# One block for three parts: routing of the last part placed inside attention's tail, weights loaded early, filler products at a seam

## The chip, the cores and the metric

The kernel runs on one core of one Trainium2 chip. The metric is the device time of one execution in microseconds (us), lower is better; the time before is the median of three runs. TensorE (PE) does matrix products and transposes, VectorE (DVE), ScalarE (ACT) and GpSimd (POOL) do elementwise work and reductions, and SyncE (SP) issues DMAs; POOL also issues DMAs. Each engine works off its own instructions in the order in which they are written, and waits on semaphores for the others.

## The reference, cut to what matters

4,096 tokens of 256 numbers pass through an expert half-step, an attention-like block, and a second expert half-step with the same weights. Cut from the reference (`ln` is a layer norm; the second line's block works on the normed rows of four sequences of 1,024):

```
x = x + 0.5 * ffn(ln(x));  x = x + attn(ln(x));  x = x + 0.5 * ffn(ln(x))

ffn(t): logits = t @ gate_w + gate_b; probs = softmax(logits)      # [4096, 8]
        e = argmax(probs)                                           # one of 8 experts
        pos = how many tokens before this one chose e               # cumsum of the one-hot mask
        keep = pos < 160                                            # capacity of an expert
        out = keep * prob_e * (gelu(t @ w1[e] + b1[e]) @ w2[e] + b2[e])

attn(x): q, k, v, g = x @ Wq, Wk, Wv, Wg; a = complex(x @ Wa) -> sigmoid(|a|) * exp(i*angle(a))
         h = scan over time: h_t = a_t * h_(t-1) + k_t * v_t;  y = (q * h * silu(g)) @ Wo
         y = ln(y + x);  out = ln(gelu(y @ W1 + b1) @ W2 + b2 + y)
```

A token's place in its expert needs the choices of all tokens ahead of it, so routing runs from the first token to the last.

## The kernel before, in words

Three functions run one after the other: `expert_half_step` (turn 0, part 1), `attention` (part 2), `expert_half_step` (turn 1, part 3). Each opens a `nc.Block` of its own and an object `Semaphores`; at its end stand a barrier over all engines, the clearing of the part's semaphores, and another barrier. The end of each engine's program in a part is a branch.

**An expert part.** Tokens lie in 32 tiles of 128 (`NT`), the slots of eight experts in ten tiles (`ST`; 8 x 160 = 1,280). Routing: DVE takes each token's best expert (`choose`: `mask`, and `seen`, a running count per partition by a scan). PE turns these into counts of earlier tokens (`count`, into `bank[3]`). DVE makes slot numbers (`place`: row within a slot tile, `row_f`; slot tile, `hot_a`; `val_tok`, the token's number at its slot tile) and then `hot`, a one-hot matrix of rows per token tile in bf16. PE sums token numbers into slots, one product per token tile (`list_tokens`), DVE makes of that the index `idx_g`, and POOL gathers ten tiles of 128 rows from DRAM by indirect DMA. In the same way mean and rstd of each row, split into three bf16 parts (`row_split`, `val_row`), go through PE into slots (`list_rows`). The gathered rows are normed (DVE), transposed (PE), and each expert takes an up-product (`up`, 32 matmuls) and a down-product (`down`, 32 matmuls). `xo` is row plus half of the gated result, and POOL scatters it into the destination by indirect DMA (the fifth and last line of the loop at L533; then POOL waits for the scatters to land).

Part 1 routes in two groups of 16 tiles, the first while later rows still load; part 3 routes all 32 tiles at once. `keep_busy(n)` issues n products of 128x512 whose result nobody reads. Part 1's second route has 10, 14, 7 and 5 of them around count and lists, part 3's route has 8, 30, 8 and 5 (L824).

**Weights.** Each expert's 2 MB lie in one of four ring slots; SP loads expert e once the down-product of e-4 is done. At part 3, expert 0 has been loaded by attention's SP program, experts 1 to 3 are loaded at part 3's own start.

**Attention.** Eight blocks (`NB`) of 512 tokens, each in two quarters of 256 for the last stages. A hand-written table of (block offset, step, number) sets the order of the work; every engine walks it and issues those of its instructions that belong to a step. `LAST_STEPS` is its end. There the last block's second stages run alone: output product `wo`, `mix_stats` and `mix_norm` (layer norm: DVE statistics, POOL's `power` chain of small operations at L1107 to L1114, DVE again), `up`, `gelu`, `split`, `down`, `out_stats`, `out_norm`, and `next_turn` and `logits`, which already make part 3's gate logits for a quarter of rows. DVE's last instruction in attention is the logits of tiles 30 and 31. L1135 is a POOL operation of `mix_norm` that adds the bias to the residual rows. The first load of attention, `zb` of `x_mid` at L1064, follows the barrier, as do seven memsets on POOL, of which the last (`rsz`) lets all other engines begin (`par_ready`). The first PE work is `z_turn` (L1530, eight transposes), then projections (L1520 to L1522).

**On-chip memory** of part 3 lay where attention's tiles had been.

## Time and profile before

| | |
|---|---|
| median of 3 runs (735.6, 735.71, 1278.68) | 735.71 us |
| profiled execution | 737.4 us, span 735.6 us |
| mean granted clock of TensorE | 0.949 |
| busy: PE, DVE, ACT, POOL | 638.0 (87%), 472.7 (64%), 453.5 (62%), 194.8 us (26%) |
| part 1 ends on DMA, POOL's last scatter | 139.59 us + landing |
| attention ends, last logits on DVE | 620.7 us |
| part 3: first filler, first expert product, last work | 624.0, 646.4, 730.9 us |

The times in the rows count from the span's start. In a timeline row stand start, busy time, engine, line, operation, output<-input, shape and count; the bracket is the idle time ahead of it and what ended that. In the windows, `PEclk` is the TensorE clock that was granted, as a share of 2.4 GHz; 0.50 is 1.2 GHz. The rows are in a section of their own below.

### The profile page before, as it was taken

What the parts mean: (1) busy time and instruction counts of PE and PEld (TensorE: products, weight loads), DVE (VectorE), ACT (ScalarE), POOL (GpSimd) and SP (SyncE); (2) the same over time, 40 slices, a digit from 0 to 9 for tenths busy, and PEclk for the clock granted to TensorE, in tenths of its full rate; (3) what the DMA queues carried; (4) which work ended last, traced back from release to release, by engine and by line L of the source; (5) the groups of instructions that cost most, each with busy time, mean ns of one, the idle gap of its engine ahead of it and who ended that gap; (6) DMA issues with size and microseconds to landing.
All of it is one profiled execution on the core that took longest, in us unless ns stands there. A gap on an engine that the chain in (4) does not pass through costs nothing. (4 is left out here: it accounts for less than half of the span.)

```text
span 735.6 us, 11483 instructions
## 1 busy us (share of the span) xinstructions
PE 638.0 (87%) x4252; PEld 566.3 (77%) x4252; DVE 472.7 (64%) x1037; ACT 453.5 (62%) x814; POOL 194.8 (26%) x289
## 2 busy tenths in 40 slices
PE   6989899456879899999999899999985995989995
PEld 3458899335668889889899798898885895479994
DVE  5664500135697989989989989988899453630001
ACT  3325334037779889898898898897896251144440
POOL 6141001221013123334234226214242221230112
PEclk9999999859879999999999999999997898899999
DMA  6939891050101201202220221011011130915720
GB/s 203 341 125 389 273 333 43 32 180 29 57 30 58 73 1 45 72 6 68 72 66 11 69 72 44 29 44 44 1 44 43 41 133 18 359 53 170 253 79 25
DMA packets 48816, 74.07 MB, mean 101 GB/s; under 512 B 4614, under 2 KB 40539, under 8 KB 48696
## 3 DMA queue, kind: packets, MB, share of 16 engines
q1 hardware_dynamic: 44408, 59.84, 24.6%
q0 software_dynamic: 4352, 13.49, 5.2%
q8 instruction: 34, 0.56, 0.3%
q14 instruction: 22, 0.18, 0.1%
HBM read 62.45 MB, written 15.20 MB: 106 GB/s over the span
## 5 line engine op out<-in xcount | busy, mean ns | idle before, releaser
L1520 PE MATMUL bank<-zt_h,w_in_h 128*128 128x512 f32 x192 | 81.1, 423 | 14.4 <-DVE qg L1207 6.1
L903 PE MATMUL bank<-xdt,ring 128*128 128x160 f32 x512 | 75.8, 308 | 5.3 <-DMA ring<-in_L_ffn_w 4.3
L1520 PE MATMUL bank<-yt_h,w_h 128*128 128x256 f32 x256 | 74.3, 290 | 6.9 <-DVE yt_l L1317 5.9
L903 PEld LDWEIGHTS bank<-xdt,ring 128*128 128x128 f32 x512 | 73.4, 197 | 6.0 <-DMA ring<-in_L_ffn_w 4.5
L1521 PE MATMUL bank<-zt_l,w_in_h 128*128 128x512 f32 x192 | 77.0, 401 | 0.0
L711 DVE SCALAR_TENSOR_TENSOR xo<-bank,gate,xg 128x256 f32<-128x256 f32 x20 | 9.2, 481 | 105.5 <-PE bank L930 105.5
L1522 PE MATMUL bank<-zt_h,w_in_l 128*128 128x512 f32 x192 | 76.8, 400 | 0.0
L1520 PE MATMUL bank<-w_h,ht_h 128*128 128x256 f32 x256 | 74.2, 290 | 0.0
L916 PE MATMUL bank<-hid,ring 128*128 128x160 f32 x512 | 72.8, 300 | 1.5 <-DVE idx_s L695 0.7
L1521 PE MATMUL bank<-w_l,ht_h 128*128 128x256 f32 x256 | 72.2, 282 | 0.0
L1522 PE MATMUL bank<-w_h,ht_l 128*128 128x256 f32 x256 | 72.2, 282 | 0.0
L916 PEld LDWEIGHTS bank<-hid,ring 128*128 128x128 f32 x512 | 70.4, 190 | 2.3 <-issue 2.3
L1521 PE MATMUL bank<-yt_l,w_h 128*128 128x256 f32 x256 | 72.1, 282 | 0.0
L1522 PE MATMUL bank<-yt_h,w_l 128*128 128x256 f32 x256 | 72.1, 282 | 0.0
L747 ACT ACTIVATE hid<-bank,b1t 128x160 f32<-128x160 f32 x128 | 50.4, 393 | 31.3 <-PE bank L903 18.3
L1107 POOL TENSOR_TENSOR rsq<-mvq,eps_ln 128x2 f32<-128x2 f32 x32 | 13.8, 430 | 208.8 <-DVE mvq L1168 208.8
L1494 ACT ACTIVATE hf<-bank,b_t 128x256 f32<-128x256 f32 x128 | 53.3, 468 | 18.2 <-PE bank L1522 13.4
L1520 PEld LDWEIGHTS bank<-zt_h,w_in_h 128*128 128x128 f32 x192 | 37.4, 195 | 25.3 <-DVE qg L1207 7.9
L1520 PEld LDWEIGHTS bank<-yt_h,w_h 128*128 128x128 f32 x256 | 48.9, 191 | 10.1 <-DVE yt_l L1317 8.0
L756 ACT ACTIVATE eot<-bank,b2t 128x160 f32<-128x160 f32 x32 | 12.6, 393 | 60.3 <-PE bank L916 60.3
L1521 PEld LDWEIGHTS bank<-yt_l,w_h 128*128 128x128 f32 x256 | 48.9, 191 | 0.7
L1521 PEld LDWEIGHTS bank<-w_l,ht_h 128*128 128x128 f32 x256 | 48.7, 190 | 0.4
(238 smaller groups left out, 1599.8 us busy)
## 6 DMA issues: line engine op xcount, KB each, us to landing
ring<-in_L_ffn_w SPq DMA_DIRECT2D x32, 1024.0 KB, 8.9
xc<-in_L_attn_x SPq DMA_DIRECT2D x8, 512.0 KB, 4.4
zb<-x_mid SPq DMA_DIRECT2D x8, 512.0 KB, 4.5
z_mid<-zb POOLq DMA_DIRECT2D x8, 512.0 KB, 3.4
zr<-z_mid SPq DMA_DIRECT2D x16, 256.0 KB, 2.8
xr<-x_mid SPq DMA_DIRECT2D x16, 256.0 KB, 3.6
out<-xq POOLq DMA_DIRECT2D x16, 256.0 KB, 4.2
xc<-in_L_attn_W SPq DMA_DIRECT2D x4, 512.0 KB, 8.4
```

The source lines that it names most:

```text
L711: V.scalar_tensor_tensor(xo[:, a % GT, :], bank[6 + a % 2][:, 0:D], gate[:, a:a + 1], xg[:, a, :], ALU.mult, ALU.add).then_inc(xo_ready, 1)
L747: S.activation(hid[:, e % 2, m, :], bank[b][:, 0:CAP], ACT.Gelu_apprx_tanh, bias=cst["b1t"][:, e * KF + m:e * KF + m + 1]).then_inc(gelu_d ...
L756: S.activation(eot[:, d, slots(e)], bank[4 + d][:, 0:CAP], ACT.Identity, bias=cst["b2t"][:, e * KD + d:e * KD + d + 1]).then_inc(eo_done, 1)
L903: ins = T.matmul(bank[b][:, 0:CAP], w1_of(s)[:, k, m * P:(m + 1) * P], xdt[:, k, e * CAP:(e + 1) * CAP], start=k == 0, stop=k == KD - 1)
L916: ins = T.matmul(bank[4 + d][:, 0:CAP], w2_of(e % GE)[:, m, d * P:(d + 1) * P], hid[:, e % 2, m, :], start=m == 0, stop=m == KF - 1)
L1107: own.step(G.tensor_tensor(rs[:], mv[:, :, 1], cst[eps][:, 0:n], ALU.add))
L1494: ins = S.activation(hf[m % 2][:, t, :], upb[m % 2][:, t * QW:(t + 1) * QW], ACT.Gelu_apprx_tanh, bias=b1_t[:, 2 * m + t:2 * m + t + 1])
L1520: T.matmul(out, left[0], right[0], start=start, stop=False)
L1521: T.matmul(out, left[0], right[1], start=False, stop=False)
L1522: return T.matmul(out, left[1], right[0], start=False, stop=stop)
```

## The change

All three parts stand in one `nc.Block`, without barriers between them. Each engine goes from its last instruction of a part to its first of the next.

- **First seam.** Attention's first load on SP waits for the five scatter semaphores of part 1 in place of the barrier. PE issues 30 fillers, waits for that load (`z_in[0]`), and issues 12 more ahead of the first transposes. POOL clears part 1's semaphores once, behind its first `z_norm` DMA.
- **Routing of part 3** is cut into tiles 0 to 25 (`EARLY`) and 26 to 31. For the first 26 the steps `choose`, `place`, `hot` and `rows` on DVE and `count`, `list_tokens` and `list_rows` on PE are new entries in `LAST_STEPS`: each takes the next piece of part 3's program, which is a generator (`yield`). The last six tiles, 26 to 31, are the second group, routed behind the last logits, with 8, 10, 4 and 5 fillers in place of 8, 30, 8 and 5.
- **Weights.** Part 3's four ring slots are now in memory that attention's first stages have left, so SP issues the loads of experts 0 to 3 behind a wait for the last block's `yg_done`, 2 MB each. What attention still uses lies below a spacer (`live`).
- Banks for counts, lists and fillers in part 3 are others than in part 1.

PE at the first seam (L916/L992 down, L930/L1006 turn_out, L1530/L1634 transposes). Before:

```order
L916 MATMUL bank<-hid,ring_0 128x160 x8
L930 MATMUL bank<-ident,eot 128x128 x4
L279 UNCONDITIONAL_BRANCH
L1513 UNCONDITIONAL_BRANCH
L1530 MATMUL bank<-ident,zb 128x128 x8
L1520 MATMUL bank<-zt_h,w_in_h 128x512
L1521 MATMUL bank<-zt_l,w_in_h 128x512
```

and now:

```order
L992 MATMUL bank<-hid,ring_0 128x160 x8
L1006 MATMUL bank<-ident,eot 128x128 x4
L1607 UNCONDITIONAL_BRANCH
L1621 MATMUL bank<-iota_p,ones_h 128x512 x42
L1634 MATMUL bank<-ident,zb 128x128 x8
L1614 MATMUL bank<-zt_h,w_in_h 128x512
L1615 MATMUL bank<-zt_l,w_in_h 128x512
```

The two branches (end of a part, start of the next) are one, and 42 fillers (L1621; 30, the wait for the load, 12) stand ahead of the transposes.

PE at the end of attention (L1607/L1608: the last product's residual; `xq`: transposes of `next_turn`; `gate_c`: logits; L814/L818: count; L834: lists). Before:

```order
L1608 MATMUL bank<-ident_r,yt_l 128x128
L1617 MATMUL bank<-ident,xq 128x128 x4
L1625 MATMUL bank<-gate_c,x3t 128x8 x4
L951 UNCONDITIONAL_BRANCH
L764 UNCONDITIONAL_BRANCH
L824 MATMUL bank<-iota_p,ones_h 128x512 x8
L814 MATMUL bank<-mask,before_m 128x256
L818 MATMUL bank<-seen,ones_h 128x256
L824 MATMUL bank<-iota_p,ones_h 128x512 x30
L834 MATMUL bank<-val_tok,hot 128x20 x32
L824 MATMUL bank<-iota_p,ones_h 128x512 x8
L834 MATMUL bank<-xo,hot 128x60 x32
```

and now:

```order
L1712 MATMUL bank<-ident_r,yt_l 128x128
L906 MATMUL bank<-val_tok,hot 128x20 x26
L906 MATMUL bank<-xo,hot 128x60 x26
L1721 MATMUL bank<-ident,xq 128x128 x4
L1729 MATMUL bank<-gate_c,x3t 128x8 x4
L895 MATMUL bank<-iota_p,ones_h 128x512 x8
L885 MATMUL bank<-mask,before_m 128x48
L887 MATMUL bank<-seen,ones_h 128x48
L889 MATMUL bank<-seen,ones_h 128x48
L895 MATMUL bank<-iota_p,ones_h 128x512 x10
L906 MATMUL bank<-val_tok,hot 128x20 x6
L895 MATMUL bank<-iota_p,ones_h 128x512 x4
```

Both lists of 26 tiles (L906) stand ahead of the last four transposes; behind the logits the branches are gone, and count (L885 to L889), fillers (L895) and lists are short.

DVE between the statistics of the last quarter's mix and those of the first quarter's output. Before:

```order
L1305 TENSOR_TENSOR vn<-bank,zr 128x512
L1164 BN_STATS stq<-vn 128x6 x2
L1166 MEMSET spare_w 128x1
L1168 BN_AGGR mvq<-stq 128x2 x2
L1164 BN_STATS stq<-bank 128x6 x2
L1166 MEMSET spare_w 128x1
L1168 BN_AGGR mvq<-stq 128x2 x2
L1336 SCALAR_TENSOR_TENSOR xq<-bank,mvq,ln2s_b 128x256 x2
```

and now:

```order
L1250 BN_AGGR mvq<-stq 128x2 x2
L656 TENSOR_TENSOR eot<-mask,bank 128x208
L657 TENSOR_REDUCE r_1<-eot 128x26
L658 TENSOR_SCALAR r_1<-r_1 128x26
L659 TENSOR_TENSOR r1i_1<-r_1 128x26
L660 TENSOR_SCALAR r1i_1<-r1i_1 128x26
L661 TENSOR_TENSOR r_1<-r1i_1,r_1 128x26
L662 SCALAR_TENSOR_TENSOR row_f<-r1i_1 128x26
L663 TENSOR_TENSOR eot<-tile_no,r_1 128x260
L665 TENSOR_TENSOR val_tok<-eot,tok 128x520
L1246 BN_STATS stq<-bank 128x6 x2
L1248 MEMSET spare_w 128x1
```

`place` for 26 tiles, nine operations (L656 to L665), stands between the two; `choose`, `hot` and `rows` stand in the same manner at three other places.

The diff, cut to its core:

```diff
-ROUTES = (((0, NT // 2), (NT // 2, NT)), ((0, NT),))
+EARLY = NT - 6
+LIVE = 4576
+ROUTES = (((0, NT // 2), (NT // 2, NT)), ((0, EARLY), (EARLY, NT)))
+ROWS = (((0, NT // 2), (NT // 2, NT)), ((0, EARLY), (EARLY, NT)))
...
+    (-1, "choose", 0), (-1, "mix_norm", 0), (-1, "mix_turn", 0), (-2, "out_stats", 1), (-1, "wo", 1),
...
+    (-1, "gelu", 3), (-1, "split", 3), (-1, "count", 0), (-1, "mix_stats", 1), (-1, "place", 0),
+    (-2, "next_turn", 1), (-1, "down", 0), (-1, "mix_norm", 1), (-1, "mix_turn", 1), (-1, "out_stats", 0),
...
+    (-1, "gelu", 5), (-1, "split", 4), (-1, "next_turn", 0), (-1, "split", 5), (-1, "hot", 0), (-1, "up", 6),
+    (-1, "up", 7), (-1, "gelu", 6), (-1, "logits", 0), (-1, "split", 6), (-1, "down", 1), (-1, "list_tokens", 0),
+    (-1, "list_rows", 0), (-1, "gelu", 7), (-1, "split", 7), (-1, "rows", 0), (-1, "out_stats", 1),
+    (-1, "out_norm", 1), (-1, "next_turn", 1), (-1, "logits", 1),
...
+        sems, sems_first = ctx.enter_context(Semaphores(nc)), Semaphores(nc)
+        block = ctx.enter_context(nc.Block())
+        first = expert_half(nc, 0, sems_first, xf, x_mid, xf, (ln1_s, ln1_b, b1), bank, cst, ring0, gate_w, gate_b, ew1,
...
+        @block.vector
+        def _(v):
+            for _ in first.vector(v):
+                pass
+        @block.tensor
+        def _(pe):
+            for _ in first.tensor(pe):
+                pass
+        def second():
+            return expert_half(nc, 1, sems, outf, outf, None, None, bank, cst, ring0, gate_w, gate_b, ew1, eb1, ew2,
+                               eb2, None, None)
...
+        if not first:
+            sb("live", [P, LIVE], F32)
+        hot = sb("hot", [P, NT * P], BF16)
...
+        tok_bank, row_bank, spare_bank = (bank[2], bank[0], bank[1]) if first else (bank[0], bank[1], bank[2])
+        count_bank = [bank[3] if first else bank[0], bank[3]]
...
-            for e in range(0 if first else 1, NE):
+            for e in range(NE):
...
-                for t in range(*ts, CT):
+            def make_hot(b, ts):
+                for g in groups(ts):
+                    n = g[1] - g[0]
+                    V.tensor_tensor(hot_group(g), cst["iota_p"][:, :, 0:n],
+                                    row_f[:, g[0]:g[1]].unsqueeze(1).to_broadcast([P, P, n]),
                                     ALU.is_equal).then_inc(hot_ready, 1)
+            def make_rows(ts):
+                for g in groups(ts):
+                    val_parts(val_row, g, slice(0, 6)).then_inc(row_val, 1)
+            def list_ids():
+                v.wait_ge(list_ready, 1)
+                own.link(V.reduce_sum(ids[:], tok_bank[:, 0:2 * ST].rearrange("p (v a) -> p a v", a=ST), AX))
+                V.tensor_copy(idx_g[:], ids[:]).then_inc(idx_ready, 1)
...
-            for b, ts in enumerate(routes):
-                if first and b:
-                    row_logits(b, ts)
-                if not first or b:
-                    choose(b, ts)
-                place(b, ts)
-                row_split(ts)
-                if b == last:
-                    v.wait_ge(list_ready, 1)
-                    own.link(V.reduce_sum(ids[:], bank[2][:, 0:2 * ST].rearrange("p (v a) -> p a v", a=ST), AX))
-                    V.tensor_copy(idx_g[:], ids[:]).then_inc(idx_ready, 1)
-                for t in range(*ts, CT):
-                    val_parts(val_row, (t, t + CT), slice(0, 6)).then_inc(row_val, 1)
+            else:
+                choose(0, routes[0])
+                yield
+            place(0, routes[0])
+            yield
+            make_hot(0, routes[0])
+            yield
+            if routes[0] in rows:
+                row_split(routes[0])
+                make_rows(routes[0])
+            yield
+            if first:
+                row_logits(1, routes[1])
+            choose(1, routes[1])
+            place(1, routes[1])
+            make_hot(1, routes[1])
+            if routes[1] in rows:
+                row_split(routes[1])
+            for ts in rows:
+                if ts not in routes:
+                    row_split(ts)
+            list_ids()
+            for ts in rows:
+                if ts not in routes[:-1]:
+                    make_rows(ts)
...
             def keep_busy(n):
-                    T.matmul(bank[1][:], cst["ones_h"][:], cst["iota_p"][:, 0:BT // CT, :].rearrange("p a b -> p (a b)"),
-                             start=True, stop=True)
+                    T.matmul(spare_bank[:], cst["ones_h"][:],
+                             cst["iota_p"][:, 0:BT // CT, :].rearrange("p a b -> p (a b)"), start=True, stop=True)
...
+                    for k, g in enumerate(parts):
+                        if t == g[0]:
+                            pe.wait_ge(ready, k + 1)
                     ins = T.matmul(out, hot_of(t), val(t), start=t == 0, stop=t == NT - 1)
                 if ts[1] == NT:
...
             else:
+                count(0, routes[0])
+                yield
+                list_tokens(routes[0])
+                yield
+                list_rows(rows[0])
+                yield
                 keep_busy(8)
-                count(0, routes[0])
-                keep_busy(30)
-                list_tokens(0, routes[0])
-                keep_busy(8)
-                list_rows(0, routes[0])
+                count(1, routes[1])
+                keep_busy(10)
+                list_tokens(routes[1])
+                keep_busy(4)
+                list_rows(rows[1])
             keep_busy(5)
...
+                if is_first(b):
+                    sems_first.clear()
...
+        ctx.close()
+        last = second()
+        block.gpsimd(last.gpsimd)
...
+                if is_first(b):
+                    for k in range(GT):
+                        sp.wait_ge(scattered[k], 16 * NG)
+                sp.dma_start(zb[b.par][:], rows).then_inc(z_in[b.par], 16)
...
+            run(sp, dict(load_z=load_z, load_quarter=load_quarter), Chain(sp, gps), 0)
+            sp.wait_ge(yg_done, 2 * NB)
+            last.sync(sp)
...
+            half = last.vector(v)
+            def choose(b, j):
+                v.wait_ge(lgq_done, 2 * (NB - 1) - (1 if EARLY < (NB - 1) * JT else 0))
+                next(half)
+            def half_step(b, j):
+                next(half)
             per_block = (2 * JT - 1) + 10 * KD
             per_quarter = (2 * QT - 1) + (3 * QT - 2) + (3 * QT - 2)
-            run(v, dict(z_stats=z_stats, z_low=z_low, fold=fold, size=size,
+            run(v, dict(choose=choose, place=half_step, hot=half_step, rows=half_step, z_stats=z_stats, z_low=z_low, fold=fold, size=size,
...
+            v.wait_ge(lgq_done, 2 * NB)
+            for _ in half:
+                pass
...
+            def keep_busy(n):
+                for _ in range(n):
+                    T.matmul(o_ffn[:], cst["ones_h"][:], cst["iota_p"][:, 0:BT // CT, :].rearrange("p a b -> p (a b)"),
+                             start=True, stop=True)
             def z_turn(b, j):
+                if is_first(b):
+                    keep_busy(30)
+                    pe.wait_ge(z_in[0], 16)
+                    keep_busy(12)
...
+            half = last.tensor(pe)
+            def half_step(b, j):
+                next(half)
             run(pe, dict(z_turn=z_turn, project=project, wo=wo, mix_turn=mix_turn, up=up, down=down,
-                         next_turn=next_turn, logits=logits), Chain(pe, actc), 0)
+                         next_turn=next_turn, logits=logits, count=half_step, list_tokens=half_step,
+                         list_rows=half_step), Chain(pe, actc), 0)
+            for _ in half:
+                pass
```

## Rows read from the trace of the kernel before

**Rows 1.** Chain that ended last, part 3's head: start us, us, what.

```profile
637.60 0.18 DVE idx_g L671
...
640.11 4.87 DMA xg<-out,idx_g
...
646.43 6.29 PE bank L903 x32
```

**Rows 2.** Timeline, PE, fillers of part 3: start us, us, what, count.

```profile
623.97 3.57 PE L824 MATMUL bank<-iota_p,ones_h 128*128 128x512 bf16 x8 [3.75 <-PEq L218]
...
637.13 1.89 PE L824 MATMUL bank<-iota_p,ones_h 128*128 128x512 bf16 x8
```

**Rows 3.** Timeline, DVE, attention's tail: last bracket is idle before, and releaser.

```profile
581.17 0.76 DVE L1164 BATCH_NORM_STATS2 stq<-bank 128x6 f32<-128x256 f32 x2 [5.64 <-PE bank L1608]
...
597.56 0.76 DVE L1164 BATCH_NORM_STATS2 stq<-bank 128x6 f32<-128x256 f32 x2 [3.32 <-PE bank L1608]
...
607.59 0.36 DVE L1364 SCALAR_TENSOR_TENSOR logits<-bank,mean_rstd,gate_b_sb 128x8 f32<-128x8 f32 x2 [1.89 <-PE bank L1625]
...
614.38 0.76 DVE L1164 BATCH_NORM_STATS2 stq<-bank 128x6 f32<-128x256 f32 x2 [5.23 <-PE bank L1608]
...
620.32 0.36 DVE L1364 SCALAR_TENSOR_TENSOR logits<-bank,mean_rstd,gate_b_sb 128x8 f32<-128x8 f32 x2 [1.81 <-PE bank L1625]
```

**Rows 4.** DMA issues of 80 to 190 us: what, count, median us to landing.

```profile
x_mid<-xo,idx_s POOLq DMA_INDIRECT x10, 2.4
```

**Rows 5.** Timeline, POOL, first seam.

```profile
139.59 0.98 POOL L533 DMA_INDIRECT x_mid<-xo,idx_s  x1 [0.30 <-issue]
...
145.99 0.10 POOL L1103 MEMSET rsz<- 128x4 f32 x1
```

**Rows 6.** Timeline, SP, first seam.

```profile
145.34 0.37 SPq L1064 DMA_DIRECT2D zb<-x_mid  x1
```

**Rows 7.** Timeline, PE, first seam, attention's transposes and first projections.

```profile
154.13 2.07 PE L1530 MATMUL bank<-ident,zb 128*128 128x128 f32 x8 [16.90 <-ACT zb L1388]
158.07 0.79 PE L1520 MATMUL bank<-zt_h,w_in_h 128*128 128x512 f32 x1 [1.87 <-DVE zt_l L1192]
...
162.06 0.40 PE L1520 MATMUL bank<-zt_h,w_in_h 128*128 128x512 f32 x1
```

**Rows 8.** Half-microsecond windows: us, PE, PEld, DVE, ACT, POOL busy, PEclk, DMA share, GB/s.

```profile
629.50:630.00 0.50, 0.50 (x4) 0.22 (x2) 0.43 (x4) 0.00 (x0) 0.00 (x0) 0.84 1.10 389
```

**Rows 9.** Timeline, DVE, part 1's second route of 16 tiles.

```profile
36.37 0.29 DVE L591 TENSOR_REDUCE r<-logits 128x16 f32<-128x128 f32 x1
...
38.16 0.42 DVE L601 TENSOR_TENSOR_SCAN seen<-not_first,mask 128x128 bf16<-128x128 f32 x1
...
39.77 0.29 DVE L609 TENSOR_TENSOR eot<-mask,bank 128x128 f32<-128x128 bf16 x1 [1.12 <-PE bank L818]
...
42.05 1.22 DVE L621 TENSOR_TENSOR hot<-iota_p,row_f 128x2048 bf16<-128x2048 bf16 x1
...
44.81 0.17 DVE L671 CAST idx_g<-ids 128x10 int32<-128x10 f32 x1
```

**Rows 10.** Timeline, PE, part 1's second lists and first expert product.

```profile
43.33 1.16 PE L834 MATMUL bank<-val_tok,hot 128*128 128x20 bf16 x16 [0.57 <-DVE hot L621]
...
51.62 4.58 PE L903 MATMUL bank<-xdt,ring 128*128 128x160 f32 x32 [0.56 <-ACT xdt L739]
```

**Rows 11.** Timeline, PE, attention's tail.

```profile
617.50 0.66 PE L1617 MATMUL bank<-ident,xq 128*128 128x128 f32 x4 [3.16 <-DVE xq L1348]
```

**Rows 12.** Timeline, POOL, late attention.

```profile
547.16 1.08 POOL L1107 TENSOR_TENSOR rsq<-mvq,eps_ln 128x2 f32<-128x2 f32 x1 [7.45 <-DVE mvq L1168]
...
594.32 0.20 POOL L1107 TENSOR_TENSOR rsq<-mvq,eps_ln 128x2 f32<-128x2 f32 x1 [7.48 <-DVE mvq L1168]
...
595.66 1.29 POOL L1135 TENSOR_TENSOR xr<-xr,ln2b_b 128x512 f32<-128x512 f32 x1
```

**Rows 13.** Two-microsecond windows, same columns, part 1's first product.

```profile
50.00:52.00 2.00, 0.82 (x5) 0.61 (x6) 1.75 (x6) 0.71 (x2) 1.70 (x2) 1.00 0.61 127
```

More of the change, by code:

```diff
@@ L210, in new, with clear @@
         return self.all[-1]
+    def clear(self):
+        self.nc.clear_and_free_semaphores(self.all)
+        self.all = []
     def __enter__(self):
@@ L288, in expert_half_step @@
         ring = [ring0] + [sb(f"ring{s}", [P, WE], F32) for s in range(1, GE)]
+        eot = sb("eot", [P, KD, GS], F32)
+        xo = sb("xo", [P, GT, D], F32)
+        mask, seen = sb("mask", [P, NT * NE], BF16), sb("seen", [P, NT * NE], BF16)
+        top, best, base, pos, late, tile_f, total, prob = [sb(f"r1{k}", [P, NT], F32) for k in range(8)]
         xg = sb("xg", [P, ST, D], F32)
@@ L893, in up @@
                 s = e % GE
-                loads = e // GE + (0 if s == 0 and not first else 1)
-                if loads:
-                    pe.wait_ge(w_in[s], loads * 32)
+                pe.wait_ge(w_in[s], (e // GE + 1) * 32)
                 pe.wait_ge(xdt_ready, -(-(e + 1) * CAP // P))
```

161 lines of the change are left out of this document (72 added, 89 removed).

## The prediction

> **What bounds the kernel now.** The table of busy time comes first: TensorE (PE) is busy 87% of the span and VectorE (DVE) 64%, so what PE does in the steady part is not touched by this change, and only places where PE waits or runs fillers can give time back. Then the chain of waits at part 3's head [rows 1]: the index `idx_g` is ready at 637.60 + 0.18 = 637.78 us, the gather beside it takes 4.87 us, and the first expert product starts at 646.43. Then the PE timeline there [rows 2]: from 623.97 on PE issues products nobody reads. Attention's last DVE instruction ends at 620.32 + 0.36 = 620.68 [rows 3]. So from 620.68 to 646.43, 25.75 us, nothing of the result is computed by PE; the length is that of barrier, route (17.1 us to the index) and gather (8.65 us from there to the first product). The first seam is the second such place: the last scatter is issued at 139.59 and lands some 2.4 us later, at 142.0 [rows 4, 5], SP's load follows at 145.34 [rows 6], and PE begins again at 154.13 [rows 7].
>
> **First seam.** The load leaves at about 142.1 in place of 145.34 (3.2 us earlier), and the last of POOL's memsets, which lets the others go, 0.75 us behind it as before (145.99 + 0.10 against 145.34 [rows 5, 6]), at 142.85. Load, norm and all up to the transposes took 154.13 - 145.34 = 8.8 us; without fillers the transposes would start at 150.9. But 42 fillers stand ahead of them. A filler takes 0.44 us at half clock, where eight took 3.57, and 0.23 at full, where eight took 1.89 [rows 2]. How long PE is at half clock after an idle stretch is between 3.9 us (158.07 to 162.06, the product's time falls from 0.79 to 0.40 [rows 7]) and 5.7 us (623.97 to about 629.66, worked out from the mean clock of 0.84 in the window that starts at 629.50 [rows 8]). I take 5.5, since here too PE starts from a long idle stretch into fillers: 12.5 fillers at 0.44 and 29.5 at 0.23 are 12.3 us, to 155.15. The fillers, not the load, then set the transposes: these take 1.04 in place of 2.07 at full clock, to 156.2, where they ended before as well. What is won is the clock of what follows: nine products that took 3.99 us [rows 7] take 9 x 0.23 = 2.1. **-1.9 us**; with 3.9 us of half clock it is -2.7.
>
> **Attention's tail.** DVE gets four pieces, each ahead of a wait that it had anyway [rows 3, 9]. `choose` with its scan took 38.16 + 0.42 - 36.37 = 2.2 us for 16 tiles, some 2.8 for 26, into an idle stretch of 5.64. `place` took 42.05 - 39.77 = 2.28 for 16, some 2.8, into 3.32. `hot` took 1.22 for 16, so 2.0, into 1.89. `rows` is an estimate: 1,560 elements at the rate of `hot` (1.22 for 2,048) are 0.95, and a dozen small operations near 0.17 each 2.0, together 3.0 to 3.1, into 5.23. In all 10.7 us into 16.1 us of idle time. Releasers stay the same, PE results in all four. PE gets a count and 52 list products; 16 took 1.16 us [rows 10], so 52 take 3.5, into an idle stretch of 3.16 ahead of 617.50 [rows 11]: 0.3 too long.
>
> POOL gets nothing, but runs beside `place`. Its small operation took 0.20 us with DVE idle and 1.08 beside DVE work [rows 12]; the chain of four that `mix_norm` waits for can so grow by up to 2.3 us of 3.32 that DVE had free, and DVE's own work can be held by the 1.29 us of L1135, which comes just behind [rows 12]. Nothing to 2.0 us for the whole tail; I take **+0.6**, 0.3 for PE and 0.3 for this, because most of the slower chain lies in the same stretch that `place` fills.
> The Trainium skill, "SBUF — State Buffer", section "Who interferes with whom", says that a VectorE instruction with two SBUF inputs contends with a GpSimd instruction that reads SBUF, and that the later of the two is fully blocked. By that rule the two-input operations of `place` and L1135 would add up instead of overlapping, and the sum below would be about 1 us higher; by the rows alone with no clash it would be 0.3 lower. The trace agrees with the rule as far as the 0.20 and the 1.08 go.
>
> The loads of experts 0 to 3, 8.4 MB, run at 389 GB/s in the window of 629.50 [rows 8], 21.5 us, and start behind the last block's `yg_done`, which lies between the mix statistics of its two quarters, 581.17 and 597.56 [rows 3]: they end between 603 and 619, before anything of part 3 reads them. Their DMA time lies beside attention's tail, which has only the output stores then. I take zero; the rival below prices it.
>
> **Second seam.** From DVE's last logits at 620.68 there is now a route of six tiles. The nearest rows are part 1's second route, of 16: 36.37 to 44.98, 8.6 us, with count and list in the same order [rows 9]. I take off 0.6 for `choose` and scan and 0.6 for `place` (a quarter each: ten of sixteen tiles are gone, but small operations hardly shrink), 0.7 for `hot`, 0.7 for ten list products at 0.07 [rows 10], and 0.4 of the 1.12 that DVE waited for the count behind ten half-clock fillers [rows 9]: 5.6 us, index at 626.3. From the index to the first product part 1 took 51.62 - 44.98 = 6.64 us [rows 9, 10], part 3 before 8.65 with ring loads beside the gather; those are gone. First product at 632.9 in place of 646.43: **-13.5**. It took 6.29 us there [rows 1] and 4.58 in part 1 [rows 10], where the clock was full [rows 13]. PE now has lists in place of the idle stretch ahead of 617.50, no barrier, and fillers as in part 1, so I take part 1's: **-1.7**.
>
> Behind it all work is the same. **Sum**: -1.9 + 0.6 - 13.5 - 1.7 = -16.5; 737.4 - 16.5 = 720.9 for the profiled execution. The median of the runs, 735.71, lies 1.7 below that execution: **719.2 us**. A measurement of this kernel tells about 2% from no change, that is anything below 721.0 or above 750.4.
>
> **Rivals.**
> - *The clock drops ahead of the first product all the same.* Between gather and product PE has nothing but four transposes, as before. Costs the 1.7: 720.9. Part 1 speaks against it, part 3 before for it.
> - *Half clock already in the short route.* If PE enters the eight fillers at 0.44 each they last 3.5 in place of 1.9 us, and the ten behind the count 4.4 in place of 2.3; both then end behind DVE: up to +3.3, 722.5. Before, PE was at half clock here, behind its idle stretch and the barrier; with lists in the stretch I doubt it.
> - *The loads disturb the tail.* 21.5 us at full DMA rate lie beside the last quarters' loads and stores; one quarter's load doubled would hold `mix` by some 3.5 to 4 us: 723.
> - *DVE's idle time is not idle when the pieces come.* The idle stretches are waits on PE, and if PE in turn waits for DVE's pieces, all 10.7 us come on top of what was taken as 0.6: 729.3. Against it: each piece stands ahead of a wait for a PE result that doesn't need the piece.
> - *PE stays at half clock through the 42 fillers.* They then last 18.5 us, transposes and nine products stay slow: +7.2 + 1.9, 728.3.
> - *Slower than before.* PE is busier at both seams, and if the chip answers with more half clock in attention, each stretch of 5.5 us at 1.2 GHz loses half, 2.75 us. Seven more of them (one per steady block) are 19.3: 738.5. It decides from six on (16.5 us). Nothing in the steady rows calls for it.
> - That the change does not do what it says would need `choose` to be held by logits of tile 25 that come late; they belong to the block before, so I give it nothing of its own.
>
> **How the numbers follow.** Forecast 0.44 (own range 716.8 to 721.5), drop ahead of the product 0.22, half clock in the route 0.12, loads 0.08, DVE not hidden 0.07, fillers at half 0.04, slower 0.03. With every small term at its good end (-0.8 at the first seam, no slip, 1 us less route) it is 716.8; with the index-to-product time of before (+2.0), the tail's full 2.0 and the drop of 1.7 it is 724.3, and a little more where the half-clock route joins one of them. Range 716.5 to 725.5; the last three cases lie outside. Below 721.0: nearly all of the forecast, half of the drop case, little else: 0.55. Above 750.4 only a heavier form of the slower case, 0.01.
>
> **What would show it.** First seam: fillers whose eighth part is 0.44 then 0.23, transposes from about 155 with no idle ahead of them, and nine products of 0.23. Tail: DVE pieces of 2.8, 2.8, 2.0, 3.1 with idle left behind the first and last; the last logits within a microsecond of before, counted from the transposes. Second seam: index 5.6 us behind the logits, gather under 4.87, product 6.6 behind the index and 4.6 long at granted clock 1.00. The prediction is wrong if the last logits come over 2 us late, if DVE waits for the count behind fillers, or if the product waits for weights.

## The result

The changed kernel takes 725.44 us (median of four, 724.42 to 725.73) against 736.07 (median of four): ratio 0.9844, 95% interval 0.9827 to 0.9862. One of the four executions of the kernel before, 1278.68 us, was in a slow state and is left out of the ratio and its interval. A second measurement (f1 below) gave 0.9882 (0.9850 to 0.9914). So it is faster, by 1.6% here and 1.2% there, but not by the 2% forecast as a little more likely than not: 719.2 us was predicted, a gain of 16.5, and 10.6 were won. The profiled execution has a span of 723.9 us, 11.7 less than before.

**First seam after the change.** PE's timeline (start, busy time, instruction, count, idle time ahead and its end), then POOL's last scatter of part 1 and SP's load:

```profile
135.75 0.66 PE L1006 MATMUL bank<-ident,eot 128*128 128x128 f32 x4 [0.48 <-ACT eot L828]
142.19 10.78 PE L1621 MATMUL bank<-iota_p,ones_h 128*128 128x512 bf16 x42 [5.79 <-POOL rsz L1143]
152.81 1.04 PE L1634 MATMUL bank<-ident,zb 128*128 128x128 f32 x8
155.81 0.50 PE L1614 MATMUL bank<-zt_h,w_in_h 128*128 128x512 f32 x1 [1.97 <-DVE zt_l L1274]
...
157.98 0.39 PE L1614 MATMUL bank<-zt_h,w_in_h 128*128 128x512 f32 x1
```

```profile
138.77 0.99 POOL L581 DMA_INDIRECT x_mid<-xo,idx_s  x1 [0.30 <-issue]
```

```profile
141.15 0.37 SPq L1212 DMA_DIRECT2D zb<-x_mid  x1
```

They answer to [rows 5, 6, 7]. The load leaves 2.38 us behind the issue of the last scatter; before, with barrier, clearing and barrier between them, it was 5.75 (139.59 to 145.34). The 42 fillers last 10.6 us up to the transposes, not 12.3; these last 1.04 us, as worked out. The nine products from the first projection to the tenth take 2.17 us (155.81 to 157.98) in place of 3.99. From the end of part 1's last transposes (136.41) to the start of the tenth product (157.98) it is 21.57 us; before it was 24.83 (137.23, the end of the transposes there, to 162.06).

**Attention's tail.** DVE's timeline, for [rows 3]:

```profile
577.80 0.76 DVE L1246 BATCH_NORM_STATS2 stq<-bank 128x6 f32<-128x256 f32 x2 [2.12 <-PE bank L1712]
...
592.40 1.28 DVE L662 SCALAR_TENSOR_TENSOR row_f<-r1i 128x26 bf16<-128x26 int32 x1
...
594.80 0.75 DVE L1246 BATCH_NORM_STATS2 stq<-bank 128x6 f32<-128x256 f32 x2
...
611.62 0.76 DVE L1246 BATCH_NORM_STATS2 stq<-bank 128x6 f32<-128x256 f32 x2 [2.17 <-PE bank L1712]
...
617.82 0.36 DVE L1446 SCALAR_TENSOR_TENSOR logits<-bank,mean_rstd,gate_b_sb 128x8 f32<-128x8 f32 x2 [2.06 <-PE bank L1729]
...
621.29 0.20 DVE L656 TENSOR_TENSOR eot<-mask,bank 128x48 f32<-128x48 bf16 x1 [1.50 <-PE bank L889]
...
625.01 0.17 DVE L685 CAST idx_g<-ids 128x10 int32<-128x10 f32 x1
```

`place` (its seventh operation, L662, stands in the second row) now fills the whole idle stretch, and the statistics behind it (594.80) start with no idle time ahead; `choose` leaves 2.12 and `rows` 2.17 us. In the route DVE waits 1.50 us for the count. PE's timeline there, for [rows 1, 2, 11]:

```profile
611.42 1.76 PE L906 MATMUL bank<-val_tok,hot 128*128 128x20 bf16 x26
613.04 1.77 PE L906 MATMUL bank<-xo,hot 128*128 128x60 bf16 x26
...
616.09 1.62 PE L1729 MATMUL bank<-gate_c,x3t 128*128 128x8 f32 x8 [0.69 <-ACT x3t L1600]
617.56 3.57 PE L895 MATMUL bank<-iota_p,ones_h 128*128 128x512 bf16 x8
...
621.08 3.37 PE L895 MATMUL bank<-iota_p,ones_h 128*128 128x512 bf16 x10
...
631.38 7.28 PE L979 MATMUL bank<-xdt,ring 128*128 128x160 f32 x32 [0.56 <-ACT xdt L811]
```

The eight fillers take 3.57 us, as at half clock before, and the first expert product 7.28. The windows of two microseconds (busy time of PE, PEld, DVE, ACT, POOL, then the granted clock, DMA share, GB/s) show why:

```profile
614.00:616.00 2.00, 1.40 (x18) 1.11 (x16) 1.68 (x7) 0.56 (x1) 0.89 (x2) 1.00 0.00 0
616.00:618.00 2.00, 1.91 (x10) 1.64 (x11) 0.18 (x2) 1.69 (x3) 0.84 (x3) 0.60 0.37 131
618.00:620.00 2.00, 2.00 (x6) 0.70 (x5) 1.59 (x9) 1.26 (x2) 0.00 (x0) 0.50 0.02 4
...
624.00:626.00 2.00, 1.89 (x20) 1.00 (x18) 1.22 (x6) 0.00 (x0) 0.53 (x1) 1.00 0.00 0
...
630.00:632.00 2.00, 1.31 (x4) 0.94 (x5) 1.83 (x8) 0.38 (x1) 1.39 (x3) 0.51 0.36 107
...
634.00:636.00 2.00, 2.00 (x9) 2.00 (x8) 0.29 (x1) 0.68 (x2) 1.42 (x2) 0.50 0.28 86
```

TensorE falls to 1.2 GHz within 616 to 618, is back at 2.4 by 624, and is low again in 630 to 636, through most of the first product.

**POOL beside `place`.** POOL's timeline, for [rows 12]:

```profile
591.38 0.69 POOL L1151 TENSOR_TENSOR rsq<-rsq,minus_half 128x2 f32<-128x2 f32 x1
...
592.30 1.33 POOL L1177 TENSOR_TENSOR xr<-xr,ln2b_b 128x512 f32<-128x512 f32 x1
```

Its chain is as quick as alone (0.69 us for the power operation), but L662 on DVE, which takes 0.18 for the same 26 tiles in f1 below, starts at 592.40 and ends at 593.68, just when L1177 (L1135 before) ends, at 593.63. In f1, the changed kernel again, L1177 starts a little earlier against DVE's sequence, and it is the operation ahead, L661, that is long:

```profile
591.71 1.29 POOL L1177 TENSOR_TENSOR xr<-xr,ln2b_b 128x512 f32<-128x512 f32 x1
```

```profile
591.71 1.33 DVE L661 TENSOR_TENSOR r<-r1i,r 128x26 f32<-128x26 int32 x1
592.96 0.18 DVE L662 SCALAR_TENSOR_TENSOR row_f<-r1i 128x26 bf16<-128x26 int32 x1
```

The same pair is there in all twelve executions with `place` in the tail: in six L661 is the long one, in six L662 (L663 and L664 in c1 to c3, e4, f2, f3). `choose` met it as well: its L646 ran beside the L1177 of the quarter before and took 1.19 us, but there 2.12 us of idle time were left behind it.

**The end.** POOL's last scatter:

```profile
715.77 0.99 POOL L581 DMA_INDIRECT out<-xo,idx_s  x1 [0.30 <-issue]
```

It is 7.14 us from its end to the end of the span at 723.9; before, it was 4.7 (735.6 less 730.9).

### The profile page after: what moved, and what is told of

It is laid out like the page before. It is cut to its first block and busy times, and to the rows that moved or that the text cites. A ratio compares the mean times of both kernels' runs of the same rounds, so it can differ in the third digit from the quotient of the medians.

```text
span 723.9 us, 11485 instructions
## 1 busy us (share of the span) xinstructions
PE 645.6 (89%) x4273; PEld 571.0 (79%) x4273; DVE 478.0 (66%) x1061; ACT 454.1 (63%) x815; POOL 196.8 (27%) x291
## 5 line engine op out<-in xcount | busy, mean ns | idle before, releaser
L979 PE MATMUL bank<-xdt,ring 128*128 128x160 f32 x512 | 77.4, 312 | 1.7 <-ACT xdt L811 1.1
L979 PEld LDWEIGHTS bank<-xdt,ring 128*128 128x128 f32 x512 | 75.0, 201 | 2.5 <-issue 1.7
L992 PE MATMUL bank<-hid,ring 128*128 128x160 f32 x512 | 72.8, 300 | 1.5 <-DVE idx_s L768 0.7
L992 PEld LDWEIGHTS bank<-hid,ring 128*128 128x128 f32 x512 | 70.4, 190 | 2.3 <-issue 2.3
```

Source lines behind the costliest of these rows:

```text
L979: ins = T.matmul(bank[b][:, 0:CAP], w1_of(s)[:, k, m * P:(m + 1) * P], xdt[:, k, e * CAP:(e + 1) * CAP], start=k == 0, stop=k == KD - 1)
L992: ins = T.matmul(bank[4 + d][:, 0:CAP], w2_of(e % GE)[:, m, d * P:(d + 1) * P], hid[:, e % 2, m, :], start=m == 0, stop=m == KF - 1)
```

## Where the time went: six stretches in all runs

Each number is a difference of rows like those above: **seam**, end of part 1's last transposes on PE to the start of attention's tenth product; **attention**, on to the end of DVE's last logits; **route**, on to the end of the cast to `idx_g`; **gather**, on to the start of the first expert product; **product**, its own time; **end**, from the end of PE's last transposes to the end of the span. All in us, one profiled execution each. What is not in a column, from the first product to PE's last transposes, is 74.7 to 74.8 us in every row but e3, where it is 78.3.

| run | part 1 | seam | attention | route | gather | product | end | span |
|---|---|---|---|---|---|---|---|---|
| before | 137.23 | 24.83 | 458.62 | 17.09 | 8.66 | 6.29 | 8.07 | 735.6 |
| changed | 136.41 | 21.57 | 460.20 | 7.00 | 6.20 | 7.28 | 10.52 | 723.9 |
| f1, changed again | 133.88 | 23.74 | 462.25 | 6.51 | 5.99 | 6.26 | 10.49 | 723.8 |
| e1, no seam fillers | 134.97 | 21.37 | 460.38 | 6.84 | 6.25 | 7.17 | 10.52 | 722.2 |
| e2, fillers for lists | 134.43 | 21.59 | 459.55 | 7.19 | 6.04 | 7.56 | 10.46 | 721.5 |
| e3, longer last fillers | 136.22 | 21.75 | 460.03 | 7.16 | 6.07 | 4.86 | 10.52 | 724.9 |
| e4, clear early | 135.96 | 21.74 | 460.26 | 7.05 | 6.17 | 7.31 | 7.31 | 720.5 |
| e5, route late | 137.26 | 23.75 | 460.41 | 19.34 | 5.99 | 6.24 | 10.52 | 738.2 |
| e6, weights late | 137.15 | 23.79 | 460.81 | 6.90 | 9.64 | 7.21 | 10.49 | 730.7 |
| c1 | 137.52 | 19.07 | 461.56 | 6.42 | 6.00 | 6.26 | 7.27 | 718.8 |
| c2 | 135.25 | 21.78 | 461.67 | 5.59 | 6.00 | 4.58 | 7.26 | 716.8 |
| c3 | 136.15 | 19.87 | 459.82 | 5.59 | 5.95 | 6.26 | 7.26 | 715.6 |
| f2, c2 again | 137.04 | 21.92 | 461.79 | 5.59 | 5.98 | 4.58 | 7.32 | 718.9 |
| f3 | 136.82 | 21.36 | 461.60 | 5.59 | 6.02 | 6.26 | 7.36 | 719.7 |

The column of part 1, which no edit touches, runs from 133.9 to 137.5, and the changed kernel's own two rows differ by 2.2 in the seam and 2.1 in attention: a difference below about 2 us in those columns is read as nothing. Much of the spread in attention is TensorE's clock. Between the second and the third of DVE's statistics in the tail lie 16.8 us at a mean granted clock of 1.00 in eight rows of the table, and 18.35 at 0.91 in the other six (f1, c1, c2, c3, f2, f3); from the third to the end of the logits it is 5.99 us at 1.00 (e2) up to 7.27 at 0.63 (e5). Over the whole column TensorE was at 1.2 GHz for 32.0 us before, 35.7 in the changed kernel and 39.0 in f1 (an estimate from the mean clock in windows of 4 us). Why the clock is low in one execution and not in the next, no run here tells. Route, gather and end repeat within 0.5 between the two executions of one kernel (changed and f1, c2 and f2).

## The experiments

**e1, no fillers at the first seam.**

```
-                    keep_busy(30)
+                    keep_busy(0)
                     pe.wait_ge(z_in[0], 16)
-                    keep_busy(12)
+                    keep_busy(0)
```

Expected: 

> The changed kernel without its 42 fillers at the first seam, all else as changed. There the first projection starts at 155.8 us in place of 158.07, and the tenth product at 158.0 in place of 162.06: 4.1 us, of which the prediction gave the barrier nothing. Theory A: the barrier's removal gives the gain and the fillers only turn it into clock; without them the transposes start near 150 us at half clock (2.07 us), the first projection near 153.5, nine products last 4.0, so the tenth product is at 157.5 to 158.5, the span within 1 us of 723.9. Rival B: the fillers give about half of the 4.1, and without them the tenth product comes at 160 or later, the span at 726.

Measured: seam 21.37 against 21.57, span 722.2, 1.7 less, of which 1.4 come from a shorter part 1. PE's timeline:

```profile
148.40 2.07 PE L1634 MATMUL bank<-ident,zb 128*128 128x128 f32 x8 [13.44 <-ACT zb L1484]
152.34 0.79 PE L1614 MATMUL bank<-zt_h,w_in_h 128*128 128x512 f32 x1 [1.87 <-DVE zt_l L1274]
```

The transposes take 2.07 us at half clock but start early enough: 13.4 us behind part 1's last transposes, and 16.4 in the changed kernel, where they wait behind the fillers. What the fillers win in clock they lose in this delay. Theory A holds: with barrier and clearing gone and no filler the seam is 3.5 us shorter than before (f3, also without fillers, has 21.36), and 42 fillers give nothing on top. In three of the seven rows with 42 (f1, e5, e6) the seam is even 23.7 to 23.8: there the clock rose later in the fillers and fell again during the nine products.

**e2, wide fillers where the lists stood.** `list_tokens` and `list_rows` of 26 tiles moved behind the last logits in place of `keep_busy(8)`; where they stood, 7 and 7 fillers.

Expected: 

> The changed kernel with the two lists of 26 tiles (52 small products) moved behind the last logits, in place of the 8 fillers there, and 14 fillers (about 3.2 us, as the lists) where the lists stood. Theory A: the clock falls to 1.2 GHz at 616.6 because the lists' products of 20 and 60 columns don't keep it up; with wide fillers there it stays at 2.4 GHz, and the route of six tiles takes 5.6 to 6.0 us from the logits to the index in place of 7.0; span about 722.5. Rival B: the transposes and logits behind it lower the clock by themselves; then it falls at the same place, the lists at half clock end no earlier than the 8 fillers did, and the index still comes 7 us or more behind the logits; span 724 or more.

Measured: the clock is at 0.95 still in 616 to 618 and the eight logits products take 1.06 us in place of 1.62, but the route is 7.19.

```profile
609.61 2.97 PE L895 MATMUL bank<-iota_p,ones_h 128*128 128x512 bf16 x13
...
614.04 1.06 PE L1730 MATMUL bank<-gate_c,x3t 128*128 128x8 f32 x8 [0.69 <-ACT x3t L1601]
614.96 1.70 PE L906 MATMUL bank<-val_tok,hot 128*128 128x20 bf16 x26
616.51 1.79 PE L906 MATMUL bank<-xo,hot 128*128 128x60 bf16 x26
```

```profile
616.00:618.00 2.00, 2.00 (x36) 2.00 (x35) 1.07 (x6) 1.73 (x3) 0.00 (x0) 0.95 0.01 4
618.00:620.00 2.00, 1.78 (x12) 0.90 (x12) 1.33 (x9) 0.00 (x0) 0.00 (x0) 0.50 0.00 0
```

The fall came late, but it came, while PE was busy with narrow list products from 615.0 to 618.3. So neither theory holds whole: wide products held the clock through the logits, and being busy with narrow ones didn't keep it from falling. No time was won in the route, as the lists stood ahead of the count where fillers had.

**e3, twelve fillers behind the last list in place of five.** `keep_busy(5 if first else 12)`.

Expected: 

> The changed kernel with 12 in place of 5 fillers behind part 3's last list, so that PE is busy until about 628.8 us, when the first gathered rows are ready to be transposed, in place of 627.2. Theory A: the thin stretch from 627.2 to 631.4 lowers the clock at 630, and so makes the first expert product 7.28 us long; with the longer filler the product takes 4.6 to 5 us and the span falls by 2.3 to 2.7, to about 721.4. Rival B: the clock falls anyway, since between 628.8 and 631.4 PE has only four transposes; the product stays over 6 us and the span within 0.7 of 723.9, or later where fillers delay the transposes.

Measured: product 4.86 us, but span 724.9. PE and ACT behind it:

```profile
631.23 4.86 PE L979 MATMUL bank<-xdt,ring 128*128 128x160 f32 x32 [0.56 <-ACT xdt L811]
...
638.45 0.35 PE L921 MATMUL bank<-val_gate,hot 128*128 128x30 bf16 x4 [0.84 <-issue]
639.88 0.24 PE L921 MATMUL bank<-val_gate,hot 128*128 128x30 bf16 x2 [1.09 <-issue]
...
641.45 5.68 PE L979 MATMUL bank<-xdt,ring 128*128 128x160 f32 x32
```

```profile
637.02 0.39 ACT L819 ACTIVATE hid<-bank,b1t 128x160 f32<-128x160 f32 x1 [1.04 <-remote]
638.46 0.39 ACT L819 ACTIVATE hid<-bank,b1t 128x160 f32<-128x160 f32 x1 [1.05 <-remote]
```

Two stops on PE of 0.84 and 1.09 us and three on ACT of 1.05, which the profile puts down to no instruction of this core, lie behind the product, and the clock fell after them (the second product took 5.68 and not 4.51 us). From the end of the first product to the start of the second it took 5.4 us in place of 3.0: stops and second product together ate more than the 2.4 us that the first had won. Nothing here tells where the stops came from. The run alone is inconclusive; c3 repeats the edit.

**e4, attention's semaphores cleared in part 3.** Attention's 69 semaphores, counted in the code, get an object of their own, cleared by POOL behind `pool.wait_ge(idx_s_ready, 1)`, where POOL waits for the first results anyway; 76 are left for the end.

```
+            if not first:
+                done_sems.clear()
```

Expected: 

> The changed kernel with attention's semaphores cleared by POOL in part 3, behind the wait for the scatter index, so that only part 3's are left for the end. From the last scatter's issue to the end of the span it took 735.6 - 730.9 = 4.7 us before and 723.9 - 716.8 = 7.1 in the changed kernel. Theory A: the clearing of two parts' semaphores at the end costs the 2.4 us, and here the end is 4.7 to 5.0 us again, the span about 721.5. Rival B: the 2.4 us have another cause (one block's end over all engines), and the end stays at 7.1.

Measured: POOL's last scatter,

```profile
715.58 0.98 POOL L583 DMA_INDIRECT out<-xo,idx_s  x1 [0.30 <-issue]
```

and a span of 720.5: 3.9 us behind it in place of 7.1; column "end" 7.31 against 10.52. Theory A: 69 semaphores more cost 3.2 us at the very end, 46 ns each, where nothing covers them. The column repeats: 10.46 to 10.52 in the seven rows that clear them at the end, 7.26 to 7.36 in the six that clear them early. The expected 4.7 to 5.0 was too high, since before the change, with the same 76 left, the end had cost 0.8 more than this (8.07 in the column); where those 0.8 went no run shows.

**c1, c2, c3, built on e4.** c1: `keep_busy(20)` and `keep_busy(10)` at the first seam. c2: besides, `keep_busy(4)` and `keep_busy(6)` in place of 8 and 10 around the last count. c3: besides, 12 fillers at the end of the route, as in e3.

Expected of c1: 

> The changed kernel with attention's semaphores cleared early, as in the run before, and 20 and 10 fillers in place of 30 and 12 at the first seam. The changed kernel's 42 fillers end 1.7 us behind attention's normed rows (ACT's last norm ended at about 151.1 us, the transposes began at 152.81). Theory A: 30 fillers end about 2.7 us earlier, still behind the clock's rise at 145.4, so that the transposes start near 150.2 and the tenth product comes 2 to 2.5 us earlier, counted from part 1's last transposes (19 to 19.5 us in place of 21.6); with the 3.4 us of the early clearing the time is 719 to 720. Rival B: the rows' norm or the clock takes over, the stretch stays at 21.0 or more, and the time is 721.5 to 722.5.

Expected of c2: 

> As c1, and 4 and 6 fillers in place of 8 and 10 around the count of the six last tiles. In the changed kernel DVE waits 1.50 us there for the count, because 8 fillers at half clock (3.57 us) stand ahead of it. Theory A: the wait goes, the index comes 5.6 to 6.0 us behind the logits in place of 7.0, and the time falls by 1.0 to 1.4 against c1. Rival B: fewer fillers leave the clock at 1.2 GHz longer, lists and transposes become slower, and no more than 0.3 us is won.

Expected of c3: 

> As c2, and 12 in place of 5 fillers behind the last list. In the run with that alone the first product fell from 7.28 to 4.86 us, but PE and ACT stood still twice for about a microsecond behind it, the clock fell at 640.7 instead, and the span was 1 us longer. Theory A: those stops belong to that one execution, and with several timed ones the 2.4 us are won against c2. Rival B: whatever holds the clock up through the first product only moves its fall to the second; then c3 is within 0.7 us of c2 or slower.

Measured: 720.93, 719.16 and 718.49 us; ratios 0.9800 (0.9735 to 0.9865), 0.9753 (0.9684 to 0.9823), 0.9753 (0.9686 to 0.9819). The three intervals overlap, so what one edit of these is worth is read from the columns. c1's time is between what its two theories said. c1's seam was 19.07, but with the same 30 fillers it was 21.78 in c2, 19.87 in c3 and 21.92 in f2: theory A's gain is there in two of four executions, and in the others the clock fell again during the nine products. c2's route is 5.59 us in both of its executions, 1.4 and 0.9 under the changed kernel's two. PE in c2, then DVE's first operation behind the count:

```profile
618.47 1.49 PE L897 MATMUL bank<-iota_p,ones_h 128*128 128x512 bf16 x3 [0.23 <-issue]
620.32 0.22 PE L887 MATMUL bank<-mask,before_m 128*128 128x48 bf16 x1 [0.36 <-DVE seen L650]
...
630.29 4.58 PE L981 MATMUL bank<-xdt,ring 128*128 128x160 f32 x32 [0.56 <-ACT xdt L813]
```

```profile
620.66 0.20 DVE L658 TENSOR_TENSOR eot<-mask,bank 128x48 f32<-128x48 bf16 x1 [0.34 <-PE bank L891]
```

The count now waits for DVE's `seen` (0.36 us) and no longer for the fillers, and DVE's wait for the count is down from 1.50 to 0.34 us: theory A for the route. The first half of rival B came true too, without its price: TensorE was at 1.2 GHz from 614.3 to 624.5 in c2 and from 616.4 to 623.2 in the changed kernel (both worked out from windows of half a microsecond). c3's product took 6.26, not 4.58, and its ratio equals c2's: rival B of c3, twelve fillers are worth nothing that shows. f3 has 6.26 with the five fillers of f2, so this column follows the clock and not this edit.

**e5, routing late.** The seven new steps for 26 tiles stand behind `(-1, "logits", 1)`, all else as changed.

Expected: 

> The changed kernel with the steps for the first 26 tiles moved behind the last logits, all else as changed: one block, early weights, same fillers. Theory A, early routing is what brings the second seam's gain: by the durations of the changed kernel's trace, choose 3.9, place 4.1, hot 2.0, row parts 3.1 us and a wait for the count come between the logits and the route of six tiles, 13 to 14 us; the tail gets back up to 1 us; time 737 to 739, that is no better than before the change. Rival B: most of the gain comes from the missing barrier and from gathering without loads beside it; then the route costs less than 8 us and the time is below 733.

Measured: 739.29 us, ratio 1.0022 (0.9995 to 1.0050). The route is 19.34 us, 12.3 longer than changed, near the 13 to 14 expected. Theory A: without the early routing nothing is left of the gain. A part of the route's 10.1 us (17.09 to 7.00) is the barrier's all the same. Before the change DVE's first routing operation waited 3.29 us behind the last logits:

```profile
623.97 0.42 DVE L591 TENSOR_REDUCE r<-logits 128x32 f32<-128x256 f32 x1 [3.29 <-PEq L218]
```

In the changed kernel it starts 0.03 us behind them. No run has the route of all 32 tiles without the barrier, so this share is read from the trace and not tested. In the tail, the first two statistics of DVE lie 16.41 us apart in e5, 16.39 before and 17.00 changed:

```profile
580.93 0.76 DVE L1248 BATCH_NORM_STATS2 stq<-bank 128x6 f32<-128x256 f32 x2 [5.83 <-PE bank L1714]
...
597.34 0.76 DVE L1248 BATCH_NORM_STATS2 stq<-bank 128x6 f32<-128x256 f32 x2 [3.32 <-PE bank L1714]
...
621.06 0.36 DVE L1448 SCALAR_TENSOR_TENSOR logits<-bank,mean_rstd,gate_b_sb 128x8 f32<-128x8 f32 x2 [2.76 <-PE bank L1731]
...
640.59 0.17 DVE L687 CAST idx_g<-ids 128x10 int32<-128x10 f32 x1
```

That is the price of `place`, 0.6 us. The other pieces cost nothing that shows: from the second to the third statistics, where `hot` and `rows` stand, it is 16.8 us with them and without, and from the tenth product to the first statistics, where `choose` stands, 419.8 us with it and 419.9 in e5.

**e6, weights late.** On SP, `sp.wait_ge(lgq_done, 2 * NB)` ahead of the four experts' loads.

Expected: 

> The changed kernel with one wait more on SP, so that experts 0 to 3 are loaded behind the last logits (near 618) and not near 583. The gathers then run beside loads as before the change (4.87 us for the tile on the chain). Theory A: the index comes as in the changed kernel, 7.0 us behind the logits; from there to the first product it takes 8.2 to 8.7 us in place of 6.2, and the time is 2 to 2.5 us longer than the changed kernel's. Rival B: the gather's share is small and the extra wait is hidden: within 0.7 us of it.

Measured: 733.13 us, ratio 0.9960 (0.9940 to 0.9979), where f1 has 0.9882. The gather stretch is 9.64 us against 6.20 and 5.99, more than theory A said, and so is the time. One gather took 6.14 us beside the loads (DMA share 1.01 to 1.11, 359 to 392 GB/s in 630 to 636), in the chain that ended last:

```profile
630.37 6.14 DMA xg<-out,idx_g
...
638.29 7.21 PE bank L979 x32
```

The same piece in the changed kernel's chain:

```profile
625.47 2.84 DMA xg<-out,idx_g
```

Early loads are worth 3.4 to 3.7 us there. The spans of e6 and f1 differ by 6.9, of which 3.3 are part 1, 3.7 the gather, 1.0 the first product, 0.4 the route and -1.4 attention, and the medians by 5.8 (733.13 less 727.32).

**f1 to f3, five rounds each on one chip.** f1 is the changed kernel, f2 is c2, f3 is c2 without fillers at the first seam.

Expected of f1: 

> The changed kernel itself, on the same chip as the next three, since the kernel before took 733 to 741 us on the chip of the combined runs and only ratios of one call compare well. Expected 0.984 to 0.985 of the kernel before, as in its first measurement.

Expected of f2: 

> The version with early clearing, 20 and 10 fillers at the first seam and 4 and 6 in the route, on the same chip as the changed kernel. Theory: end -3.2, first seam -2.5 to 0 (it took 19.1, 19.9 and 21.8 us with 30 fillers, 21.4 to 21.8 in most with 42), route -1.3: 4.5 to 7 us under the changed kernel, ratio to the kernel before 0.975 to 0.978.

Expected of f3: 

> As f2 without any filler at the first seam. Theory A: the fillers there are worth nothing: without them transposes start as soon as the rows are normed, at half clock, and the tenth product came 21.4 us behind part 1 against 21.6 with 42; then f3 is 0 to 2.5 us slower than f2 and not faster. Rival B: the fillers only shift where the clock is low, and f3 equals f2 within 0.5 us.

Measured: f1 727.32, ratio 0.9882 (0.9850 to 0.9914), f2 720.80, 0.9765 (0.9730 to 0.9801), f3 720.92, 0.9784 (0.9753 to 0.9816). f1 came out above the 0.984 to 0.985 expected. f2 is 6.5 us under the changed kernel, as expected, the best version here together with c2 and c3; that any of them gains more than 2% is not shown, as each interval reaches beyond 0.98. f3 and f2 overlap, and the seam took 21.36 without and 21.92 with fillers: rival B, they only shift where the clock is low.

## Why the prediction was only half right

The time, 725.44 us, lay 0.06 inside the upper end of the range, 725.5, and the second measurement, 727.32, outside it: that the range held is luck. The forecast's own range, 716.8 to 721.5, did not hold. Two rivals, each priced by itself, came true together, and a term that was left out came on top. The sum of -16.5 us stood against -11.7 in the profiled execution. By its steps, with what each missed:

- **First seam, -1.9 forecast, -3.3 measured, -1.1 in f1.** In this execution the nine products did win 1.8 by the clock, as forecast. The other 1.4 came because PE was at half clock for 3.2 us of the fillers and not for the 5.5 taken, so that they ended earlier; in f1, e5 and e6 it was 4.8 to 5.8. But the gain was put down to the wrong part of the change: I gave it all to the fillers, and e1 shows that without barrier and clearing, and without a filler, the gain is 3.5; the fillers add nothing.
- **Tail, +0.6 forecast, +1.6 measured.** `place` is 0.6 (e5): it lasted from 590.8 to 594.9, 4.1 us and not 2.8, because one of its operations was held beside POOL's L1177 for 1.1 us; without that it would have been 3.0, less than the 3.32 that were free. PE's 0.3 were nothing: the last transposes start 3.12 us behind the third statistics in both kernels. (By its own row, 16 list products in 1.16 us, 52 are 3.8 us and not 3.5; they took 3.4.) `choose` took 3.9 us and not 2.8, hidden by idle time. Of the rest, 0.3 is the last stretch with the logits products at a lower clock (0.86 against 0.90), and 0.7 lies ahead of the first statistics; e5, without any piece there, has 0.8, so it is not the pieces', and its cause stays open. The POOL chain that I feared for was not slowed.
- **Route, 5.6 us forecast, 7.0 measured (6.5 in f1).** This is the rival "half clock already in the short route": it came true with 1.4 of its 3.3 us. Its reasoning, that lists in the idle stretch would keep the clock, failed: the lists ran back to back from 611.4 to 614.8, and at the logits products, behind an idle gap of 0.69 us, the clock fell. The 5.6 itself was right: c2 measures 5.59 with four fillers ahead of the count, which end before DVE's `seen`, and at half clock.
- **Gather, 6.64 us forecast, 6.20 measured.** Right, and e6 shows the cause: 9.64 with loads beside it. The step "loads hidden in the tail, zero" held: with them at 355 to 404 GB/s beside it in 600 to 606, the tail from the second to the third statistics took 16.82 us, as before.
- **First product, -1.7 forecast, +1.0 measured.** The other rival, "the clock drops ahead of the first product", came true too, and harder than priced. That PE resembled part 1 there was no proof: its time is 4.58, 4.86, 6.2 to 6.3 or 7.2 to 7.6 over the fourteen executions, by where a low stretch begins (630.0 to 636.9 in the changed kernel, across the product; in c2 it ended at 624.5 and none followed before the product's end).
- **"Behind it all work is the same", 0 forecast, +2.4 measured.** A term that was left out. The description of the kernel before had said that each part clears its own semaphores; in one block attention's 69 are cleared at the end with part 3's, 3.2 us by e4. That it came to 2.4 is because the end was otherwise 0.8 us shorter than before, for a reason that no run shows.

Misses: 0.8 for part 1, 1.4 at the seam, 0.4 at the gather and 0.1 in what no column holds to the good; 1.0 in attention, 1.4 in the route, 2.7 at the first product and 2.45 us at the end to the bad: 4.8 together, the gap of 16.5 to 11.7. The steps that failed are thus the clock through the route and the first product, the end, and the tail.

The Trainium skill, "SBUF — State Buffer", section "Who interferes with whom", was weighed against a slip of 0.3 us without it: a two-input VectorE operation and a GpSimd operation that reads SBUF block one another, the later one fully. This case's trace agrees: whichever two-input operation of `place` is issued while L1177 runs ends within 0.1 us of the end of L1177, after 1.28 us and 1.33 in place of 0.18 or 0.19. Its price, about 1 us, is that of the delay, 1.1; but DVE had some idle time left, so that the statistics came 0.6 later, which is nearer to the 0.3 that I had taken.

## What to carry to other kernels

When barriers go, ask where their work goes: the clearing of semaphores moved to the uncovered end and cost a fifth of the gain; put it where the engine waits anyway. Products put in to keep an engine awake stand in its queue: ahead of the one result that another engine waits for, 8 held it up and 4 did not (c2, where those behind the count also went from 10 to 6). A term that rests on which clock a short stretch will have gets both prices and even chances, since it differed between two executions of the same kernel; and rivals that can come true together get the sum of their prices as well.

## What the runs showed of the hardware

- A DVE operation with two inputs in SBUF on 128x26 elements that takes 0.2 us took 1.3 us where POOL was adding two 128x512 tiles in SBUF; both ended within 0.1 us, in twelve executions.
- Being busy did not hold TensorE at 2.4 GHz: in e2, with 52 products of 20 and 60 columns back to back from 614.96 to 618.30, the granted clock was 0.95 in 616 to 618 and 0.50 in 618 to 620.
- The same kernel does not get the same clock each time: the seam took 21.57 and 23.74 us, and the 32 products of the first expert 7.28 and 6.26, in two executions of the changed kernel.
- Clearing 69 semaphores more at the end of the program took 3.2 us (10.52 against 7.31).
- An indirect gather of 128 rows took 6.14 us beside loads at 359 to 392 GB/s and 2.84 without them; from index to first product it took 9.64 and 6.20 us.
